# Sixteen pairs of experts joined on chip, and a down projection in three float32r products

## The reference

```python
topk_idx, topk_w = _gate(x, gate_w, gate_bias)          # 4 experts of 32 for each token
buf = jnp.zeros((E, CAP, H)).at[flat_e, slot].set(x_rep, mode='drop')
h = jax.nn.silu(jnp.einsum('ech,ehf->ecf', buf, w1)) * jnp.einsum('ech,ehf->ecf', buf, w3)
ob = jnp.einsum('ecf,efh->ech', h, w2)                  # the down projection
y = ob[flat_e, jnp.minimum(slot, CAP - 1)]
y = jnp.where(keep[:, None], y, 0.0)
out = (y.reshape(n, K, H) * topk_w[:, :, None]).sum(1)
return (out + shared).reshape(b, s, h)
```

## Time and profile before

| what | value |
|---|---|
| median of 3 runs | 1021.8 us (1020.78 to 1023.94) |
| the profiled execution, whole | 1017.46 us |
| its span (what the profile shows) | 1015.7 us |
| mean granted clock of PE, as a share of full speed | 0.96 |
| busy share of the span | PE 91%, DVE 57%, ACT 34%, POOL 30% |
| the expert loop | 794.0 us to the end of the span |

### The profile page before, as it was taken

One profiled execution on the slowest core, in us unless ns is written; L12 is line 12 of the kernel. 1 busy time (PEld: TensorE's weight loads), 2 busy tenths in 40 slices (PEclk: granted clock), 3 DMA queues, 4 the chain that ended last, 5 costly groups with the idle time before them and its releaser, 6 DMA issues.

```text
span 1015.7 us, 16393 instructions
## 1 busy us (share of the span) xinstructions
PE 927.6 (91%) x6224; PEld 563.3 (55%) x6224; DVE 583.2 (57%) x1335; ACT 346.8 (34%) x699; POOL 299.9 (30%) x304
## 2 busy tenths in 40 slices
PE   5777999999999999999999999799999899999993
PEld 4535546645754764764674674364777444444441
DVE  1346846886786795795786687684352233332221
ACT  4021064265246336326417425417200112112220
POOL 4002001110520540341251153042323243336564
PEclk9699599799999999999999999999999999999997
DMA  5373203302300500520330330280513799999642
GB/s 142 70 269 100 48 3 84 84 3 68 100 24 26 132 14 2 148 63 3 99 90 24 79 89 3 63 291 2 195 55 94 281 349 305 293 305 309 140 50 27
DMA packets 99618, 114.91 MB, mean 113 GB/s; under 512 B 12141, under 2 KB 76327, under 8 KB 99536
## 3 DMA queue, kind: packets, MB, share of 16 engines
q1 hardware_dynamic: 83908, 94.42, 30.0%
q0 software_dynamic: 12176, 16.30, 8.1%
q10 hardware_dynamic: 3456, 3.15, 1.2%
HBM read 70.90 MB, written 16.88 MB: 86 GB/s over the span
## 4 chain that ended last, share of the span: by engine, by line
PE 70%; DVE 17%; ACT 5%; issue 4%; DMA 2%; SPq 0%; POOL 0%; ACTq 0%; POOLq 0%; DVEq 0%
PE qa L1718 11%; PE qa L1571 6%; DVE mxx L1071 6%; PE qx L1705 5%; PE qa L1365 4%; PE pt L1283 4%; PE qx L1509 4%; PE vb L1520 4%; PE qa L1283 4%; PE qx L1451 4%; ACT arena L680 3%; PE qa L1399 2%; DVE mx L1039 2%; PE pt L1684 1%; PE vb L1354 1%
## 5 line engine op out<-in xcount | busy, mean ns | idle before, releaser
L1071 DVE TENSOR_REDUCE mxx<-qx 128x2 f32<-128x512 f32 x256 | 168.3, 685 | 45.1 <-PE qx L1451 43.8
L680 ACT ACTIVATE arena<-qx 128x512 f32<-128x512 f32 x256 | 146.4, 602 | 127.4 <-PE qx L1509 111.7
L680 ACT ACTIVATE arena<-qa 128x512 f32<-128x512 f32 (+2 forms) x125 | 67.2, 540 | 211.3 <-PE qa L1718 117.4
L516 POOL TENSOR_TENSOR rstd<-mv,power 128x2 f32<-128x2 f32 x24 | 17.2, 717 | 368.8 <-DVE mv L907 368.8
L1718 PE MATMUL qa<-arena 128*128 128x512 f32 x256 | 116.9, 600 | 1.1 <-ACT arena L680 1.1
L1451 PE MATMUL qx<-arena 96*128 96x256 bf16 x512 | 103.9, 293 | 13.8 <-DVE mxx L1071 9.6
L1509 PE MATMUL qx<-arena 98*128 98x512 bf16 x256 | 94.5, 391 | 6.9 <-ACT arena L680 2.9
L1520 PE MATMUL vb<-arena 128*32 128x256 f32 x1024 | 82.2, 393 | 1.6 <-ACT arena L680 0.4
L1451 PEld LDWEIGHTS qx<-arena 96*128 96x128 bf16 x512 | 46.9, 102 | 57.8 <-DVE mxx L1071 26.2
L1718 PEld LDWEIGHTS qa<-arena 128*128 128x128 f32 x256 | 47.4, 192 | 52.2 <-issue 52.2
L1230 DVE SCALAR_TENSOR_TENSOR arena<-arena,qa 128x256 f32<-128x256 f32 x32 | 13.5, 421 | 102.7 <-ACT arena L680 102.7
(11 more groups left out here) (223 smaller groups left out, 1611.3 us busy)
## 6 DMA issues: line engine op xcount, KB each, us to landing
arena<-in_L_ffn_w SPq DMA_DIRECT2D x96, 512.0 KB, 6.6
qs<-arena SPq DMA_DIRECT2D x24, 384.0 KB, 5.0
arena<-arena SPq DMA_DIRECT2D x72, 128.0 KB, 3.5
res<-in_x SPq DMA_DIRECT2D x8, 512.0 KB, 6.8
xnd<-arena SPq DMA_DIRECT2D x8, 512.0 KB, 5.9
ks<-arena SPq DMA_DIRECT2D x48, 64.0 KB, 1.9
arena<-arena SPq DMA_DIRECT2D x48, 64.0 KB
arena<-arena ACTq DMA_DIRECT2D x24, 128.0 KB, 3.6
```

The costliest lines, as they stand in the source:

```text
L680: nc.scalar.activation(dst, src, func, **kw).then_inc(s[signal], 1)
L1071: v_.reduce_max(mxx[:, col:col + 3:2], xbank[v % 2].rearrange("p (h n) -> p h n", h=2), AX.X).then_inc(s["x_max"], 1)
```

## The change

Three things change together.

1. `PAIRED` goes from 16 to all 32 experts. The column halves, `half_ids` and the semaphores `y_out` are gone. `spread_ids` and `shared_tokens` become float32r products. Since float32r keeps fewer bits than float32, the odd expert's weighted rows are split into a rounded part and a remainder (`split_second`: `y_hi`, `y_lo`), and two products are added up. The id matrix and the 0/1 matrix are held in one buffer each instead of two.
2. `shared_tokens` and `join_pair` move by one step: from the even step after the pair to the odd step after it, where PE does `shared_tokens` between `bring` and `down`, and DVE does `join_pair` last. `ids_out` moves from the even step to the odd step before.
3. The down projection is computed from operands split in the same way: `w2_hi` and `ht_hi` are rounded on ACT, `w2_lo` and `ht_lo` are the remainders, computed on DVE (`split_down`). Three products, hi·hi, hi·lo and lo·hi, each in two chunks, make six float32r matmuls of 512 columns in place of two float32 ones. The split operands have one buffer each, in the memory of `qs` and `ks`, which attention used. So the splits of expert e wait until `down(e-1)` has read them.

```diff
-PAIRED = 16
+PAIRED = NE
...
-ABSENT = 65535
+ABSENT = 4095
...
-        id_diag = [view(arena, 3 * WCOLS + r * P, P) for r in range(2)]
-        same = [view(arena, ht_at + DC * S + 2 * F + r * P, P) for r in range(2)]
-        assert 3 * WCOLS + 2 * P <= fetch_at
-        half_ids = sb("half_ids", [P, 2, NE], U32)
+        f32r = qs[:].rearrange("p h n -> p (h n)")
+        ones_r = view(f32r, 0, P)
+        id_diag = view(f32r, P, P)
+        same = view(f32r, 2 * P, P)
+        y_hi, y_lo = (view(f32r, 3 * P + r * D, D) for r in range(2))
+        w2_hi = view(f32r, 3 * P + 2 * D, 2 * D).rearrange("p (c n) -> p c n", c=2)
+        ht_hi = view(f32r, 3 * P + 4 * D, 2 * P).rearrange("p (c n) -> p c n", c=2)
+        f32r_too = ks[:].rearrange("p a h n -> p (a h n)")
+        w2_lo = view(f32r_too, 0, 2 * D).rearrange("p (c n) -> p c n", c=2)
+        ht_lo = view(f32r, 3 * P + 4 * D + 2 * P, 2 * P).rearrange("p (c n) -> p c n", c=2)
...
-            for e in range(PAIRED, NE):
-                pool.wait_ge(s["y_ready"], e + 1)
-                for h, side in enumerate(y_out):
-                    if e > PAIRED:
-                        pool.wait_ge(side, (e - PAIRED) * 16)
-                    nc.gpsimd.indirect_dma_start(
-                        flat, bass.IndirectOffsetOnAxis(ap=half_ids[:, h, e:e + 1], axis=0),
-                        ye[e % YR][:, h * (D // 2):h * (D // 2) + D // 2], None,
-                        bounds_check=2 * N - 1, oob_is_err=False, compute_op=ALU.add).then_inc(side, 16)
-                if e + FETCH < NE:
-                    fetch(e + FETCH)
-            for side in y_out:
-                pool.wait_ge(side, (NE - PAIRED) * 16)
...
+                if e > 0:
+                    act.wait_ge(s["down_done"], e)
+                act.wait_ge(wg_in[e % EU], e // EU * 48 + 48)
+                copy(w2_hi, h2[e % EU], "w2_hi")
                 act.wait_ge(s["ht_t"], e + 1)
-                if e >= 2:
-                    act.wait_ge(s["down_done"], e - 1)
-                copy(hte[e % 2], va[:, 0:2 * P].rearrange("p (c n) -> p c n", c=2), "ht_ready")
+                copy(ht_hi, va[:, 0:2 * P].rearrange("p (c n) -> p c n", c=2), "ht_hi")
...
-                if YR <= e < PAIRED + YR:
+                if e >= YR:
                     dve.wait_ge(pair_out[(e - YR) % 2], (e - YR) // 2 * 16 + 16)
-                elif e >= YR:
-                    for side in y_out:
-                        dve.wait_ge(side, (e - YR - PAIRED + 1) * 16)
                 v_.tensor_scalar(ye[e % YR], xbank[0], iw[:, e * 2 + 1:e * 2 + 2].bitcast(F32), None, ALU.mult
                                  ).then_inc(s["y_ready"], 1)
 
+            def split_down(e):
+
+                if e > 0:
+                    dve.wait_ge(s["down_done"], e)
+                dve.wait_ge(s["w2_hi"], e + 1)
+                v_.tensor_tensor(w2_lo, h2[e % EU], w2_hi.bitcast(F32), ALU.subtract).then_inc(s["w2_split"], 1)
+                dve.wait_ge(s["ht_hi"], e + 1)
+                v_.tensor_tensor(ht_lo, va[:, 0:2 * P].rearrange("p (c n) -> p c n", c=2), ht_hi.bitcast(F32),
+                                 ALU.subtract).then_inc(s["ht_ready"], 1)
+
             def ids_out(i):
 
                 dve.wait_ge(s["id_t"], i)
-                v_.tensor_scalar(id_diag[i % 2], ident[:], id_f[:, 2 * i:2 * i + 1], None, ALU.mult
+                v_.tensor_scalar(id_diag, ident[:], id_f[:, 2 * i:2 * i + 1], None, ALU.mult
                                  ).then_inc(s["id_diag"], 1)
 
             def same_tokens(i):
 
                 dve.wait_ge(s["id_t"], i + 1)
-                dve.wait_ge(s["twice_t"], max(i - 1, 0))
-                link(v_.tensor_scalar(same[i % 2], vb[:, 0:P], id_f[:, 2 * i + 1:2 * i + 2], None, ALU.is_equal))
-                link(v_.reduce_sum(twice[:], same[i % 2], AX.X))
+                dve.wait_ge(s["twice_t"], i)
+                link(v_.tensor_scalar(same, vb[:, 0:P], id_f[:, 2 * i + 1:2 * i + 2], None, ALU.is_equal))
+                link(v_.reduce_sum(twice[:], same.bitcast(F32), AX.X))
                 link(v_.scalar_tensor_tensor(once_f[:], twice[:], float(2 * N), id_f[:, 2 * i + 1:2 * i + 2],
                                              ALU.mult, ALU.add))
                 v_.tensor_copy(once[:, i:i + 1], once_f[:]).then_inc(s["same"], 1)
 
+            def split_second(i):
+
+                y = ye[(2 * i + 1) % YR]
+                dve.wait_ge(s["y_ready"], 2 * i + 2)
+                dve.wait_ge(s["twice_t"], i)
+                v_.tensor_copy(y_hi, y).then_inc(s["y_hi"], 1)
+                dve.wait_ge(s["y_hi"], i + 1)
+                v_.tensor_tensor(y_lo, y, y_hi.bitcast(F32), ALU.subtract).then_inc(s["y_split"], 1)
+
...
             dve.wait_ge(s["iw_in"], 16)
+            v_.tensor_copy(ones_r, ones[:])
             link(v_.tensor_copy(id_f[:], iw[:].rearrange("p (e c) -> p e c", c=2)[:, 0:PAIRED, 0]))
+            ids_out(0)
...
                 if e > 0:
                     weigh_out(e - 1)
-                if e % 2 == 0 and e < PAIRED:
-                    ids_out(e // 2)
+                if e % 2 == 0 and 0 < e <= PAIRED:
+                    split_second(e // 2 - 1)
                 if e % 2 == 1 and e < PAIRED:
                     same_tokens(e // 2)
-                if e % 2 == 0 and 0 < e <= PAIRED:
+                if e % 2 == 1 and e + 1 < PAIRED:
+                    ids_out(e // 2 + 1)
+                split_down(e)
+                if e % 2 == 1 and 1 < e <= PAIRED + 1:
                     join_pair(e // 2 - 1)
             weigh_out(NE - 1)
+            split_second(PAIRED // 2 - 1)
+            join_pair(PAIRED // 2 - 1)
...
-                mm(vb[:, 0:P], ones[:], id_diag[i % 2], start=True, stop=True).then_inc(s["id_t"], 1)
+                mm(vb[:, 0:P], ones_r, id_diag, start=True, stop=True).then_inc(s["id_t"], 1)
 
             def shared_tokens(i):
 
                 pe.wait_ge(s["same"], i + 1)
-                pe.wait_ge(s["y_ready"], 2 * i + 2)
+                pe.wait_ge(s["y_split"], i + 1)
                 pe.wait_ge(s["pair_ready"], i)
-                mm(xbank[1], same[i % 2], ye[(2 * i + 1) % YR], start=True, stop=True).then_inc(s["twice_t"], 1)
+                mm(xbank[1], same, y_hi, start=True, stop=False)
+                mm(xbank[1], same, y_lo, start=False, stop=True).then_inc(s["twice_t"], 1)
 
             def down(e):
+                pe.wait_ge(s["w2_split"], e + 1)
                 pe.wait_ge(s["ht_ready"], e + 1)
                 if e > 0:
                     pe.wait_ge(s["y_ready"], e)
                 for c in range(2):
-                    op = mm(xbank[0], hte[e % 2][:, c, :], h2[e % EU][:, c, :], start=c == 0, stop=c == 1)
+                    mm(xbank[0], ht_hi[:, c, :], w2_hi[:, c, :], start=c == 0, stop=False)
+                    mm(xbank[0], ht_hi[:, c, :], w2_lo[:, c, :], start=False, stop=False)
+                    op = mm(xbank[0], ht_lo[:, c, :], w2_hi[:, c, :], start=False, stop=c == 1)
                 op.then_inc(s["down_done"], 1)
...
                 if e + 1 < NE:
                     bring(e + 1)
+                if e % 2 == 1 and 1 < e <= PAIRED + 1:
+                    shared_tokens(e // 2 - 1)
                 if e > 0:
                     down(e - 1)
...
-                if e % 2 == 0 and 0 < e <= PAIRED:
-                    shared_tokens(e // 2 - 1)
             down(NE - 1)
+            shared_tokens(PAIRED // 2 - 1)
```

More of the change, by code:

```diff
@@ L278, in build @@
             xnd_out t3_t xt3_ready g_t th_ready chosen dve iw_in
-            pos_t slot_ready sdat_ready half_ids init_out sc_out
+            pos_t slot_ready sdat_ready init_out sc_out
             sh_gu sh_th sh_free sh_sig sh_ga sh_h sh_down sh_added
-            id_diag id_t same twice_t pair_ready xe_t xe_tr up_done th_done ga_done h_done ht_t ht_ready down_done y_ready""".split()
+            id_diag id_t same y_hi y_split twice_t pair_ready w2_hi w2_split ht_hi xe_t xe_tr up_done th_done ga_done h_done ht_t ht_ready down_done y_ready""".split()
         s = {n: sem(n) for n in names}
@@ L285, in build @@
         wg_in = [sem(f"wg_in{r}") for r in range(EU)]
-        y_out = [sem("y_out_left"), sem("y_out_right")]
         pair_out = [sem("pair_out_first"), sem("pair_out_second")]
@@ L640, in _ @@
                 fetch(e)
-            flat = out.rearrange("b s (h d) -> (b s h) d", h=2)
-            for h in range(2):
-                nc.gpsimd.tensor_scalar(half_ids[:, h, :], ids[:, :, 0], 2.0, float(h), ALU.mult, ALU.add
-                                        ).then_inc(s["half_ids"], 1)
-            pool.wait_ge(s["half_ids"], 2)
             whole = out.rearrange("b s d -> (b s) d")
```

## The result

| | before | after |
|---|---|---|
| median | 1021.3 us (1014.5 to 1023.9, 4 runs) | 1009.3 us (1004.3 to 1010.8, 4 runs) |
| ratio | | 0.989 (0.986 to 0.993) |
| profiled execution, whole | 1017.46 us | 1010.77 us |
| its span | 1015.7 us | 1008.9 us |
| the first up ends at | 799.4 us | 805.0 us |

The kernel became 1.1% faster. The forecast was 1006.0 us and the range 1001 to 1015. I call the last two rows together "the loop": 216.3 us before, 203.95 after, 12.4 us less. The span shows only 6.8 us less, because this execution reached the loop 5.6 us later, through code that is the same in both kernels. The first experiment is about that.

The account below looks back on a forecast made before the run. PE was taken to bound the expert loop. Fourteen pairs of 11.28 us and three single steps put the last up 22.6 us earlier; the tail takes 7 back, leaving 15.8 less: 1006.0 us, range 1001 to 1015.

Parts of the forecast that it names:

- a float32r record: On PE, 512 columns in down and shared tokens: bounded at 0.21 to 0.24 us, taken as 0.2135, against 0.43 for float32.
- the pair: Two expert steps on PE: 11.28 us, from 5.48 even and 5.80 odd, against 13.79 and 11.62 before.
- the 22.6 us that I forecast for PE: Expert loop: the last up ends at 973.6 us instead of 996.2, 22.6 us earlier.
- DVE and ACT within the step: Expert loop: DVE delivers 0.55 and 0.3 us early in odd steps, 0.8 in even; PE stays the bound.
- Rival B: Odd steps: hand-overs exceed DVE's slack, each 0.1 us beyond costing 1.6 us; at 0.5 beyond, 1014 us. Chance 0.12.
- The tail: Behind the last up: the last pair waits for a 4.5 us landing; span ends at 999.9, taking back 7 us.
- Rival C: DVE waits for POOL's DMA issue on shared ports in even steps, 11 us over sixteen pairs: 1017 us. Chance 0.05.
- Rival D: Transfers reach 372 GB/s; landings of adding DMAs grow to 9.5 us and bound the first nine pairs: 1015. Chance 0.05.
- E: Down and shared tokens on PE: a float32r record takes 0.43 us like float32, 48.5 us more: 1054. Chance 0.05.
- F: Whole expert loop: the pairing or the split does not pay, some 1 us a pair of unseen wait: 1021. Chance 0.07.
- The absolute time: Whole kernel: the profiled execution goes from 1017.5 to 1001.7 us, the median to 1006.0.

Follow-up runs that it names:

- The first experiment: The kernel after run again with no edit: loop 203.9 us, first up beginning at 794.7 us instead of 801.3; median 1004.2 us against 1015.0, ratio 0.990.
- cols256: The kernel after with each down projection product as two of 256 columns, twelve records a step for six: loop 205.5 us, 1.5 more than after.
- more_dve: The kernel after with two unused DVE subtractions added to each step, about 1.0 us: loop 215.9 us, 1018.2 us in one run.
- moved_back: The kernel after with the shared tokens and the join back in the even step: loop 233.0 us, 1031.2 us in one run.
- mixed: The kernel after with experts 16 to 31 in column halves as before, gathers 11 ahead: loop 207.2 us, ratio 0.991 (0.988 to 0.994).
- Run 5: The kernel after with experts 16 to 31 in column halves as before, the same run as mixed: loop 207.2 us, ratio 0.991.
- pairs_only: The kernel after with the down projection of before, in two float32 products without splits: loop 213.1 us, ratio 0.999 (0.995 to 1.002).
- split_only: The kernel before with only the down projection of after, in three float32r products: loop 215.3 us, ratio 1.000 (0.997 to 1.003).

## Why the prediction came out as it did

**The failed term: a float32r record.** I took 0.2135 us, near the low end of 0.21 to 0.24. It is 0.229. Fourteen records a pair at 0.015 more are 0.22 us of the 0.23 by which the pair missed (11.51 for 11.28). Over the loop 208 such records (180 of down, 28 of the shared tokens) lie between the end of the first up and that of the last. At 0.0155 each they make up 3.2 of the 3.5 us between 174.2 and 177.75. The chain of before had the answer in its 0.24. I preferred half of a float32 record, which no float32r row showed. It wasn't the fixed cost of a record that I left out, for by `cols256` that is 0.01 at the most. The rest goes with the columns. So of the 22.6 us that I forecast for PE 19.1 came.

**DVE and ACT within the step: right.** `y_hi` took 0.43 (upper bound 0.69), `w2_lo` 1.22, `ht_lo` 0.42, `w2_hi` on ACT 1.06. PE waits for DVE only in the first step and at the end. The slack is 0.67 and 0.49 where I had 0.55 and 0.3, and the slower records made part of that. By `more_dve` 1 us more a step uses it up, and by `moved_back` the place of the pair's work is worth more than the change. Rival B fell.

**The tail: right.** It should be 26.3 us (999.9 less 973.6) and is 26.2. The landing took 4.16 us (4.5), and from the last issue to the end it took 10.97 (10.7). The tail takes back 6.7 of PE's 19.1 us.

**Rival C, half right, and at no cost here.** POOL and DVE do get in each other's way, but what waits is POOL's issue, not DVE. In after POOL's issue at 864.99 started 0.01 us ahead of `y_lo` and 0.64 ahead of `w2_lo`, and neither side took longer:

```profile
864.99 1.56 POOL L654 DMA_INDIRECT out<-arena,once  x1 [0.31 <-issue]
```
```profile
865.00 0.71 DVE L1219 TENSOR_TENSOR qs<-arena,qs 128x512 fp32r<-128x512 f32 x1
865.63 1.21 DVE L1191 TENSOR_TENSOR ks<-arena,qs 128x1024 fp32r<-128x1024 f32 x1
```

In `mixed` the subtraction started first, and the issue took 2.46. The 32 `w2_lo` of after took 1.21 to 1.23 us each throughout. Its issues took up to 1.78 us, two of them with `y_lo` begun 0.36 us ahead, and PE didn't wait for that. The Trainium skill, "SBUF — State Buffer", on the shared port pair, says that whichever of the two starts first keeps the pair for the whole instruction and the other blocks. Run 5 agrees for POOL as the second, and the two rows above disagree for DVE as the second. I had read the earlier trace rows wrongly. There the DVE operation had started 0.18 us ahead of the issue, so that its unchanged 0.41 us doesn't contradict the Trainium skill's rule and says nothing of a DVE operation that comes second. The issue took 1.19 us, where the median of its group is 0.98, which looks like a small case of what run 5 shows. The row of the addition has a DVE operation with only one tensor input, so it doesn't bear on operations with two.

**Rival D fell by less than I gave it.** Landings grew to 8.0 us at the worst, and the pair's loop on POOL to 10.7 of 11.51. That the 369 GB/s disagrees with the 358 was a misreading: the same section of the Trainium skill, "Perfetto Trace Analysis", Engine Utilization (under Roofline), gives the 358 as a core's share when both cores of a pair are active, and says that one core alone can pull more. **E and F fell** with the rows above. The F in the expectation of `cols256` is another one, the fixed cost of a record.

**The absolute time.** The profiled execution is 9.0 us above the 1001.7 that I worked out: 3.5 from the records, nothing from the tail, and 5.6 from a loop that began later. I had taken the start from the one profile of before and allowed for it only by the spread of before's runs, though it varies by 14 us from one execution to the next. That the median, 1009.3, missed by only 3.3 us is partly luck. The first up, too, that I called slow "as before" (5.38 us) took 3.7 in after and in the second profile of before. The granted clock was 0.68 from 794.0 to 799.4 us in the first profile of before, and 1.00 around the first up of the second. That was this execution, not the kernel.

**What I didn't see.** I priced the joining of the second half by PE alone, where it costs: a quiet pair takes 11.62 us before and 12.19 in `pairs_only`. What it brings is on POOL. In `before` the halves had caught up with a step of 5.81 us by the end; in `mixed` and `split_only`, with a step of 5.48, they had not. How much of the change is that? `split_only` (loop 215.3), `mixed` (207.2) and after (203.95) are the steps on the way. The split with the pairs as they were brings 1.0 of the 12.4 us, the move of the first half's pair work (with its products in float32r) another 8.1, and the joining of the second half the last 3.3. The medians can't tell `mixed` (0.991) from after (0.989, and 0.990 in the second round), so the joining of the second half is shown by the loops of single profiles alone.

## What to carry to other kernels

Walk the engines through one period, each operation by its row, and say how much slack each hand-over has: here that met the idle times within 0.2 us. Where a kernel becomes faster on its bounding engine, look at the chain of writes behind it that just kept up: in `split_only` it took back 9.0 of the 9.9 us that PE had won. Parts of a change don't add up, so measure them in steps, each on top of the last. Compare profiles from a point behind the noisy stretch, and take a duration from a row of the same kind of operation (0.24) before you take half of another kind's.

## What the runs showed of the hardware that I had not expected

- A float32r matmul of 128x128 by 512 columns holds the array for 0.229 us, one of 256 columns for 0.12, with weight loads hidden. A float32 one of 512 columns takes two records of 0.43.
- An indirect DMA's issue on POOL takes 1.54 us. It takes 2.44 to 2.48 when a DVE operation with two SBUF inputs (1.23 us) started 0.16 to 0.20 us ahead of it, and ends some 1.4 us behind the end of that operation. If POOL starts first, DVE isn't delayed (0.71 and 1.21 us).
- The stretch ahead of the loop varies by 14 us between executions of the same code. 6.6 us of it are stalls of PE before small matmuls that wait for nothing the profile shows, in one execution; the rest goes with the granted clock of the first 200 us, 0.83 to 0.89.
